# Key block 3 as one score tile over both query halves, and four value-product visits a quad in place of six

## The reference

```python
kv_c = x @ W_kv; kv_c = kv_c * rsqrt(mean(kv_c**2) + EPS) * g_kv
q_c = x @ W_q
k_content, v = heads(kv_c @ W_kdec, 16), heads(kv_c @ W_vdec, 16)
q_content = heads(q_c @ W_qdec, 16)
k_rope, q_rope = heads(x @ W_krope, 32), heads(q_c @ W_qrope, 32)   # both rotated by cos/sin
q, k = concat(q_content, q_rope), concat(k_content, k_rope)         # 16 heads of 48
scores = einsum('bhqd,bhkd->bhqk', q, k) * 48 ** -0.5               # causal mask over 1024 x 1024
out = einsum('bhqk,bhkd->bhqd', softmax(scores), v) @ W_o
```

## Time and profile before

| | us |
|---|---|
| median of 3 runs | 1963.67 |
| lowest, highest | 1953.01, 1965.78 |
| the profiled execution: its own time | 1961.27 |
| its span in the profile | 1959.6 |
| TensorE (PE) busy | 1901.9 (97%) |
| VectorE (DVE) busy | 1434.8 (73%) |
| ScalarE (ACT) busy | 1013.1 (52%) |
| GpSimd (POOL) busy | 858.1 (44%) |

### The profile page before, as it was taken

The page is one execution under the profiler, slowest core; times in us unless marked ns, Lnnn a source line. Parts: engine busy times, 40 slices in busy tenths (PEclk is TensorE's granted clock), DMA queues, the critical chain, the costliest instruction groups (busy, mean ns, idle before and its releaser), DMA issues.

```text
span 1959.6 us, 32772 instructions
## 1 busy us (share of the span) xinstructions
PE 1901.9 (97%) x11102; PEld 1337.0 (68%) x11102; DVE 1434.8 (73%) x4570; ACT 1013.1 (52%) x2125; POOL 858.1 (44%) x912
## 2 busy tenths in 40 slices
PE   8789999999999999999999999999999999999997
PEld 7546666767767676776767677677766777677556
DVE  5667777777777777877877777777778778677632
ACT  3435565555555555555555555545555555554551
POOL 3456454543445435355452545535444543432121
PEclk9879999999999999999999999999999999999999
DMA  3775675676775656766666676755677566665611
GB/s 104 199 191 155 166 188 151 151 187 167 176 177 129 178 149 159 200 157 153 162 164 152 179 189 156 179 149 153 153 189 178 143 158 174 167 147 129 133 41 44
DMA packets 169767, 307.50 MB, mean 157 GB/s; under 512 B 15104, under 2 KB 33792, under 8 KB 169600
## 3 DMA queue, kind: packets, MB, share of 16 engines
q1 hardware_dynamic: 169600, 305.40, 62.3%
HBM read 178.99 MB, written 126.22 MB: 156 GB/s over the span
## 4 chain that ended last, share of the span: by engine, by line
PE 86%; DVE 8%; ACT 3%; issue 2%; DMA 1%; POOL 1%; SPq 0%; POOLq 0%; DVEq 0%
PE st_b L775 15%; PE mx_b L807 15%; PE st_b L777 13%; PE o_b L795 13%; PE tp_b L843 5%; PE wj_b L732 5%; PE tp_b L840 4%; PE wj_b L719 3%; PE wj_b L701 3%; PE wj_b L734 2%; PE wj_b L712 2%; PE wj_b L741 1%; PE wj_b L747 1%; DVE mx_b L998 1%; ACT probs L884 1%
## 5 line engine op out<-in xcount | busy, mean ns | idle before, releaser
L884 ACT ACTIVATE probs<-st_b 128x512 f32<-128x512 f32 (+3 forms) x1536 | 699.6, 490 | 582.2 <-PE st_b L777 535.8
L998 DVE CUSTOM_DVE_ANT_0 mx_b<-mx_b,tri 128x256 f32<-128x256 f32 (+3 forms) x1024 | 510.6, 516 | 123.8 <-PE mx_b L807 120.5
L775 PE MATMUL st_b<-st 97*128 97x512 f32 (+2 forms) x1536 | 587.7, 388 | 8.5 <-ACT probs L884 5.0
L807 PE MATMUL mx_b<-st 96*128 96x256 f32 (+2 forms) x1536 | 543.2, 400 | 23.8 <-DVE mx_s L998 14.3
L777 PE MATMUL st_b<-st,k_st 96*128 96x512 f32 (+2 forms) x1536 | 531.2, 350 | 0.0
L1001 DVE TENSOR_REDUCE mx_s<-mx_b 128x1 f32<-128x512 f32 (+1 forms) x512 | 334.3, 653 | 131.8 <-PE mx_b L807 126.5
L1199 POOL TENSOR_SCALAR_AFFINE_SELECT probs<-probs 128x512 f32<-128x512 f32 x256 | 172.2, 677 | 538.1 <-ACT probs L884 538.0
L807 PEld LDWEIGHTS mx_b<-st 96*128 96x128 f32 x1536 | 280.9, 192 | 181.1 <-issue 73.4
L775 PEld LDWEIGHTS st_b<-st 97*128 97x128 f32 x1536 | 291.4, 190 | 123.8 <-issue 54.7
L777 PEld LDWEIGHTS st_b<-st,k_st 96*128 96x128 f32 x1536 | 294.2, 192 | 37.1 <-issue 13.9
L795 PE MATMUL o_b<-probs,v_s 128*17 128x512 f32 (+3 forms) x3072 | 290.3, 496 | 0.0
(11 more groups left out here) (198 smaller groups left out, 2332.7 us busy)
## 6 DMA issues: line engine op xcount, KB each, us to landing
st<-q_scratch SPq DMA_DIRECT2D x128, 384.0 KB, 6.0
st<-k_scratch SPq DMA_DIRECT2D x128, 384.0 KB, 8.7
k_st<-k_scratch SPq DMA_DIRECT2D x128, 384.0 KB, 9.2
q_scratch<-hi_t SPq DMA_DIRECT2D x32, 768.0 KB, 3.8
q_scratch<-lo_t SPq DMA_DIRECT2D x32, 768.0 KB, 5.3
k_scratch<-hi_t SPq DMA_DIRECT2D x30, 768.0 KB, 6.1
k_scratch<-lo_t SPq DMA_DIRECT2D x30, 768.0 KB, 4.9
ao_scratch<-o_f SPq DMA_DIRECT2D x252, 32.0 KB, 1.8
```

The lines of the kernel that those rows point to most:

```text
L775: nc.tensor.matmul(dst, k1_st[u][0:SHIFT + 1, a, P * j:P * j + P], q_st[u][0:SHIFT + 1, a, q0:q0 + w], start=True, stop=False)
L807: nc.tensor.matmul(mx_b[:, m % 2, 0:w], q_st[u][0:SHIFT, a, P * i:P * i + P], k1_st[u][0:SHIFT, a, k0:k0 + w], start=True, stop=True).then ...
L884: nc.scalar.activation(probs[:, a, PLACE[s]:PLACE[s] + n], st_b[:, a % 2, HALF - n:HALF], ACT.Exp, scale=SCALE).then_inc(exp_done, 1)
L998: nc.vector.tensor_tensor_reduce(src, src, tri[:, HALF - n:HALF], 1.0, NEG, ALU.add, ALU.max, dst).then_inc(mx_done, 1)
```

## The change

1. The tile of key block 3 in half 0 is widened from 128 to 256 columns (queries 384 to 639, so over the edge of the two halves), and the tile of key block 3 in half 1 shrinks from 512 to 384 columns (queries 640 to 1023). That second tile is moved up from place 7 to place 5, behind the tile of key block 0 in half 1. The 12 tiles have now 512, 384, 256, 256 | 512, 384, 512, 512, 512, 384, 256, 128 columns; the sum stays 4608.
2. PV has four visits: tiles (0, 1, 2, 3), (4, 5), (6, 7, 8), (9, 10, 11). The new list TAKES says what a visit multiplies. The part of tile 3 that belongs to half 1 (128 columns) is multiplied in the second visit, after tile 4, which starts the sums of that half. So tile 3's place in the ring is free only after the second visit (PV_OF).
3. The first score of tile 3 now waits for the shift of half 1 as well (shift_in[u][1]).
4. The last job's first output products wait in addition until o_b is read and all exponentials are done.
5. All order tables are new. TensorE's has 3940 letters (head 1120, batch 478 four times, tail 908) with the same S, X, F, J, P; 128 V in place of 192, 45 d in place of 68.

```diff
+BOTH = HT - 1
 ATT = []
 for h2 in range(2):
     for j in range((h2 + 1) * HT):
         q0 = max(P * j, HALF * h2)
-        ATT.append((h2, j, q0, HALF * (h2 + 1) - q0, q0 == P * j))
+        if j == BOTH:
+            q0 += P * h2
+        ATT.append((h2, j, q0, HALF * (h2 + 1) - q0 + (P if j == BOTH and not h2 else 0), q0 == P * j))
+
+at = [s for s in range(len(ATT)) if ATT[s][0] and ATT[s][1] == BOTH][0]
+ATT.insert(HT + 1, ATT.pop(at))
...
-PV = [(s, s + 1) for s in range(0, NS, 2)]
+PV = [(0, 1, 2, 3), (4, 5), (6, 7, 8), (9, 10, 11)]
 NV = len(PV)
-PV_OF = [p for p in range(NV) for _ in PV[p]]
-PV_END = [max(p for p in range(NV) if ATT[PV[p][1]][0] == h2) for h2 in range(2)]
+TAKES = []
+for p in range(NV):
+    takes = [(s, ATT[s][0], ATT[s][2], min(ATT[s][3], HALF * (ATT[s][0] + 1) - ATT[s][2])) for s in PV[p]]
+    if HT in PV[p]:
+        takes.insert(1, (BOTH, 1, HALF, P))
+    TAKES.append(takes)
+PV_OF = [max(p for p in range(NV) if s in [take[0] for take in TAKES[p]]) for s in range(NS)]
+PV_END = [max(p for p in range(NV) if ATT[PV[p][-1]][0] == h2) for h2 in range(2)]
...
                     if late and k == 0:
                         pe.wait_ge(ao_early, 16)
+                        pe.wait_ge(o_read, 2 * QUADS)
+                        pe.wait_ge(exp_done, UNITS * QUADS)
...
                     if j == 0 and a == 0:
                         pe.wait_ge(shift_in[u][h2], 16 * (g // 2 + 1))
+                    if s == BOTH and a == 0:
+                        pe.wait_ge(shift_in[u][1], 16 * (g // 2 + 1))
...
-                    for s in PV[p]:
-                        h2, j, q0, n, _ = ATT[s]
+                    for s, h2, q0, n in TAKES[p]:
+                        j, place = ATT[s][1], PLACE[s] + q0 - ATT[s][2]
                         for a in range(HQ):
                             last = nc.tensor.matmul(o_b[32 * a:32 * a + DV + 1, 0, q0 - HALF * h2:q0 - HALF * h2 + n],
-                                                    v_s[g // NQ % 2][:, j, HQ * q + a, :], probs[:, a, PLACE[s]:PLACE[s] + n],
+                                                    v_s[g // NQ % 2][:, j, HQ * q + a, :], probs[:, a, place:place + n],
                                                     start=(j == 0), stop=(s == PV[PV_END[h2]][-1]))
```

More of the change, by code:

```diff
@@ L150 @@
[L150 to L159, removed]
@@ new lines @@
+        "JXSSXXJXSXSJXSXSPSXSXVXSXSPSXSXFXSSXPSXSXPSXSXVSXSXPSXSXPSXSXSSXSSXXSXSFXSSXPSXSXPXSXSJXSXSJXSXSJXSXSJXX"
+        "VXXPSSXVXSXSXSXSXSXSXSXSJXSSXJXSXSJXSSXVFSSXXSSXXSSSXSXVSXSXJSXSJXSSXJXSXSJXSXSPSXSXFSXSXPSXSXJXSXSXPXSS"
+        "XXJXSXSJXSXSVXXPSXSXVXSXSPXSXSXJXSXSJXSXSJXSXSJXSSPSVSFSXXSPSXSXPSXSXJSXSXJSXSXJSXSXPSXSXPSXSXVSFSSPXSXS"
+        "XSSXPXSXSXVXSXSXPXSXSPSXSXSVXSXSJXSXSXJXSJXSXSJXSXSXSXSXSSVXSXSXSSXJSXSJFSXSXJSX",
+        "SXSXVXSXSXSXSXSXSXSSSXSXSSJSSXJXSSXJFXSXSXJXSXSPXSXSPXSXSJXXPVXXJXSXSJXSXSVXSXSPXSXSXPXSXSPSXSXJSXSXJSSJ"
@@ new lines @@
+        "XSXSJXSXSPXXSSXFXSSXVXXPVSXSXJSXSPXSXSJXSXSJSXSXPSXSXFSXSXPSXSXSXSPXSXSSXSXXSXSVXJXSJXSXSJXSXSJXSXSXVXSX"
+        "SXPXSXSPXSXSJXSXSJFSSXJSXSXVSXSXSXSXSXSXSVSXSXJSXSXJSSXJXSXSJFSXSXPSXSXPSXSXJXSXSXPXSSXXJXSXSJXSXSVXXPSX"
+        "SXVXSXSPXSXSXJXSXSJXSXSJXSXSJXSSPSVSFSXXSPSXSXPSXSXJSXSXJSXSXJSXSXPSXSXPSXSXVSFSSPXSXSXSSXPXSXSXVXSXSXPX"
+        "SXSPSXSXSVXSXSJXSXSXJXSJXSXSJXSXSXSXSXSSVXSXSXSSXJSXSJFSXSXJSX",
+        "SXSXVXSXSXSXSXSXSXSSSXSXSSJSSXJXSSXJFXSXSXJXSXSPXSXSPXSXSJXXPVXXJXSXSJXSXSVXSXSPXSXSXPXSXSPSXSXJSXSXJSSJ"
@@ new lines @@
+        "CEEJEEEEHECEECEECEEJEEJEEJEEHEJEJEECEECEEEEJEECEEEEEECCEEEEEEEEEHEEEECEEEEECEEJJEECJEEHEEJEECEEJEECEEEEC"
+        "EEEEEEHEECEECEEEEEEEECEEJEEJEHEJEECEEEECEEJEECEEJCEEEECEEEEHEECEEJEEEEEEEECEECEEEEEEEEEEEHEEEEEEEJEEJEEJ"
+        "EEJEECEEEEJEEEEEEEECEEEECEEEEEEHEECEEEEEEEEJEEJEEJEEJEEJEECEEJEEEEHEECEEEECEEEECEECEEEECEECEEEEEEEEHEECE"
+        "ECEEJEEJEEJJHJEECEEEEEEEEEEJEEEEEEEEEEEEEEEEJEEJEEJEEJEECEEEECEEJEECEEEEHEECEEEECEEJEEJEEJEEJEEHEJCEEECE"
+        "ECEEJEEEEEECEECEEEEECEEEEHEECEECEECEEEEEJEHEEJJEEJEEEEEEJEEEEJEEEE",
@@ new lines @@
+        "EEEEEEEEEEEEEEEJEEJEEJEEJEECEECJCEEEHEEEEECEECEECEEJEEJEEJEEJHEECEEJEECEEJEECEEEEEECEEEECEEEEEEHEEEEJEJC"
+        "EEJEEJEJEEECEECEEJEEEEHEEEEEEEEEEEJEEJEEJEEJEECEECEEJEECEEEEHEECEEEECEEJEEJEEJEEJEEHEJCEEECEECEEJEEEEEEC"
+        "EECEEEEECEEEEHEECEECEECEEEEEJEHEEJJEEJEEEEEEJEEEEJEEEE",
+        "EEEEEEEEEEEEEEEJEEJEEJEEJEECEECJCEEEHEEEEECEECEECEEJEEJEEJEEJHEECEEJEECEEJEECEEEEEECEEEECEEEEEEHEEEEJEJC"
+        "EEJEEJEJEEECEECEEJEEEEHEEEEEEEEEEEJEEJEEJEEJEECEECEEJEECEEEEHEECEEEECEEJEEJEEJEEJEEHEJCEEECEECEEJEEEEEEC"
@@ L211 @@
+        "EECEEEEECEEEEHEECEECEECEEEEEEHEEEEEEEEEEEEEJEJEJEEJEEEEJEEEEEEEEEJEEEEEEEEEEEEEEEEEEEEEEEEEEEEJEEJEEJEEJ"
+        "EEJEEEEEJEEEEEEEEEEEEEEEEEEEEEEEEEEEEEEEEEEEEEEEEEEEEEEEEEEEEEEEEEEEEEEEEEEEEEEEEEEEEEEEEEEEEEEEEEEEEEEE"
+        "EEEEEEEEEEEEEEEEEEEEEEEEEEEEEEEEEEEEJJEEJJEEEEJEEEJjjjjjj",
     ),
@@ new lines @@
+        "MMMMLJoMMoJoMoMMMMMMMMMMJMMJMMMMfMJnMMJMMJMMJJMMJooMoMoMMLMMfLMMJnMMJMMoMMooMMoMMMMMMJJJJJJMMJJJJMMMMMMJ"
+        "MMJMMMMLLMMfMMnMMMMMMooMJMJMMJoMMoMMLfMMnMMLJMMJMMMMMMMMMMJJJJoMMJoMJoJoMMJMJMMJMMLMMLMJMMJMMfJJJnMMJMMJ"
+        "MMooMoMoMMMMMMMJfMMnJMMMMMJMMMLMMJMMLMMJJJMMJoooMMJJMMoMMMMMMMMMMJfJJJJJLJLnMMJJJMMMMMMJMMJMMMMMMfonoooM"
+        "MLMMMMLMJJMJMMoJMMJMMoLooMMMMMMLMMMJMMJMMJJJJJJJJMMMMMfJnMMJ",
+        "MJMMJoMMJMoMMJMMJMMoMMoMfnMMMMMJMMJMMMMJLoMMooJMMoLMMJJJMMJMJMMJMMMMLMMMMMMfJMMJnMMJJMJLJJJMMJJooMoMMoMM"
@@ new lines @@
+        "JMMJMMfMMnMMMLMMJJJMMMMJMMJLMMoMMooMMoMJMMJJJJMJMMJJJJMMMMLMMfJnMJMMJJLJMMMMJMMJoMMooMMoMMMfnMMJMMJMMMJM"
+        "MMLMMJMMLMMJJJMMJoooMMJJMMoMMMMMMMMMMJfJJJJJLJLnMMJJJMMMMMMJMMJMMMMMMfonoooMMLMMMMLMJJMJMMoJMMJMMoLooMMM"
+        "MMMLMMMJMMJMMJJJJJJJJMMMMMfJnMMJ",
+        "MJMMJoMMJMoMMJMMJMMoMMoMfnMMMMMJMMJMMMMJLoMMooJMMoLMMJJJMMJMJMMJMMMMLMMMMMMfJMMJnMMJJMJLJJJMMJJooMoMMoMM"
+        "JMMJMMfMMnMMMLMMJJJMMMMJMMJLMMoMMooMMoMJMMJJJJMJMMJJJJMMMMLMMfJnMJMMJJLJMMMMJMMJoMMooMMoMMMfnMMJMMJMMMJM"
@@ L262 @@
+        "sJqskasuusuaqkJusqsakJJssuuaqkusuksqJsasJuuauuqkss",
+        "qJkasJJsuauqkuqsuaskJsJsuuaqkssJuuqaksJJsuuaqkusuksqJsasJuuauuqkss",
+        "qJkasJJsuauqkuqsuaskJsJsuuaqkssJuuqaksJJsuuaqkusuksqJsasJuuaJuuqksqskaJsJsJaqkqsaksJJssaqkqsaksssaksskaa"
+        "JjjaJj",
     ),
```

125 lines of the change are left out of this document (28 added, 97 removed).

## The result

| us | before | after |
|---|---|---|
| median (lowest to highest, runs) | 1963.82 (1953.01 to 1965.78, 6) | 1949.16 (1944.84 to 1952.39, 6) |
| the profiled execution: time, span | 1961.27, 1959.6 | 1944.84, 1943.1 |

The account below looks back on a forecast made before the run. TensorE's own instruction stream was taken as the bound. The terms -15 - 20.5 + 0.9 + 0.65 = -34 us took the profiled 1961.3 to 1927.3, carried as 1928 us; range 1912 to 1949.

Parts of the forecast that it names:

- Part 1: Tiles of key block 3: 256 TensorE score matmuls 128 columns shorter, 15 us off; masks and row maxima unchanged.
- the ScalarE sum: ScalarE's exponentials of the two key block 3 tiles: 873 ns before, 877 after, counted as nothing.
- Part 2: Value products on TensorE: six visits a quad become four, 64 fewer at 0.32 us each, 20.5 us off.
- A further group of tiles: Added tile group within visits: 0 to 0.065 us each, taken as 0, with 10 us kept at the range's upper end.
- Part 3: New letter order on TensorE: 0.9 us for leaving other work, 0.65 us more in the tail, alternation 0.
- rival D: Alternating scores and row maxima removes a third of TensorE's 57.7 us idle time, 19 us: 1908 us; chance 0.07.
- Part 4: Added waits on tile 3's shift, its mask and the last job: taken as 0, upper bound 3 us.
- A: Visit cost of 0.32 us belongs to tile groups or returns as gaps, only the tiles' gain remains: 1948 us; chance 0.08.
- B: VectorE takes over in stretches as longer visits empty the row maxima banks; half the gain returns as waits: 1944; chance 0.09.
- C: First visit waits for tile 3's mask in GpSimd's queue, stopping TensorE; at 2 us a quad 1991 us; chance 0.03.
- The ring: Places of exponentials: the first visit must free tile 6's; tightest cover before the third score 0.86 us; taken as 0.
- the sign of being wrong: TensorE idle time on L775 or L807 behind ScalarE, VectorE or a DMA growing by more than 15 us.

Follow-up runs that it names:

- e1: New score tiles, TAKES and waits on the kernel before, with six visits and the old order tables except the front of quad 0: 1959.11 us, 0.9992.
- e4: Changed kernel with row maxima and scores in pairs again, XSXS written XXSS at 400 places of TensorE's table: 1966.48 us, 1.003 to the kernel before.
- e2: Changed kernel (new tiles, four visits) on the old order, only TensorE's V letters moved: 2140.01 us, 1.0932 to the kernel before.
- e3: Changed kernel in its new order with six visits of two tiles, 64 V letters put back: 2185.01 us, 1.1121 to the kernel before.
- both cuts: Exponentials and row maxima over half their columns from quad 2 on: kernel before 1931.26 us (0.9842), changed kernel 1919.59 us (0.9787).

## Why the prediction was wrong, point by point

**Part 1, the tiles: right in size, 15 us.** The distances are 0.235, 0.177 and 0.12 us as forecast, and the distances of e1 are 15 us shorter in sum. But alone it brings no gain that can be measured: "Masks and row maxima stay as they are" and the ScalarE sum, right as durations, say nothing of when a bank comes free.

**Part 2, the visits: right.** One slip: the four-tile visit has 1280 columns, not 1408, since tile 3's other 128 go with the second visit; it takes 2.28 us, by the same line. A further group of tiles costs nothing like 0.065 us.

**Part 3, the letters: not confirmed.** I took 0 for alternation and gave it a chance of its own downward, rival D, which didn't come. But e4 costs 17 us, so in these tables alternation does give something, mostly by fewer held matmuls (17 us of cost; the idle time of e4 is only 5 us larger) and not by taking from the 57.7 us of idle time as I had thought. With the pairs of e4 the whole gain is gone. That the measured time is still below before rests in part on a term that I had put at nothing.

**Part 4 is the step that failed.** "I take 0, with 0.1 us a quad or 3 us as the upper bound of an ordinary miss": I asked only whether a new wait would be long, and took for granted that all old waits stay. In its place the traces have 23 us in held matmuls, 151 more of them, 0.7 us a quad. The mechanism that I lacked is that a matmul costs 0.1 us as soon as its release comes at its turn. The two banks keep the exponential and the maximum two letters ahead; that more of them come just in time where the stream between becomes shorter is my reading, which e1 bears out (28 more) and no run isolates. By releaser, the exponentials' share rose by 11 us, that of the row maxima by 7, that of the evacuations of the projections' bank by 4.

**The rivals.** A's time, 1948, was the nearest. Its first half, that the constants aren't the visit's, is excluded by the rows of the visits; its second, that they "come back as gaps because the work behind is not ready any sooner", says in words what happened, and I gave the two together 0.08. B (1944, half of the gain back as waits) had the sum nearly right. Its mechanism is only a part: VectorE is the releaser of a third, and taking half of its maxima away left the pair closer together, not wider. C did not come in the change; the first visit stands 1.35 us (median) behind its mask, and TensorE idled before two of the 128 visits for a mask, 0.9 us in all. The ring isn't it either, although it changed as Part 4 feared. ScalarE waited for visits as follows, before (first row) and after:

```profile
ACT probs L884 <- PE o_b L795: 29.6, 12, 4.0
```

```profile
ACT probs L860 <- PE o_b L771: 63.0, 27, 4.0
```

That is ScalarE waiting 33 us more for TensorE, while TensorE's own waits behind these visits are some 0.03 us in the mean.

**What I had named as the sign of being wrong** (idle time on the score and maxima lines up by 15 us) did not show: it went from 32.3 to 32.7. Two other signs did: busy time is down by 17.6 in place of 34, and two visits show waits on the masks, though only 0.9 us. A wait that is shorter than the overlap of two matmuls is counted as busy, so idle time can't find it.

**What is shown and what is open.** Shown: the counted gain is in the stream; some 23 us come back in matmuls released just in time; the changed kernel has more of these at four loads of the other engines and at three orders of TensorE's table. Not shown: that the gain would be there without them, for no version got rid of them, and why just these letters. That a shorter stream under unchanged chains of two banks makes more of them is argued, with e1 for it; a third bank of st_b or mx_b wasn't tried. No version that does all of the work beat the changed kernel.

## What to carry to other kernels

Where TensorE is the bound and each step waits on a bank that two steps share, count what carries a wait and how far ahead its release comes, not only how long the waits are: each one that is released less than 0.1 us ahead costs up to 0.1 us behind it, beside what it is late itself. The page's idle and busy times don't show this loss; start-to-start times do, and here it took more than half of what the stream was cut by. An order found on a replay of one trace is a conjecture until it has run, even where the replay meets that trace within 1%.

## What the runs showed of the hardware that was not expected

- A matmul that starts at its release makes the next one 0.104 us late, however short its own wait; with 0.05 us of lead this is 0.05, from 0.11 us on nothing (the table above, for scores behind exponentials; for row maxima only the first of these is shown). The rows at 790.78 and 791.11 show one.
- Where TensorE waited more, its granted clock was lower, so that waits cost more than their length. The mean was 0.984 in the kernel before, 0.953 in e2 and 0.939 in e3 (above), where visits stood for masks and matmuls for maxima. Of spans of 1959.6, 2141.9 and 2193.9 us this takes an estimated 31, 101 and 134 us. With both cuts in the changed kernel it was 0.992 (1913.7 us of span). The Trainium skill, page "TensorE: Matmul & The Clock Gate", section "HAM oscillation — how this bites in real kernels", tells of a kernel whose clock falls in each wait for a DMA; the runs agree in so far as the clock is lower with more waits, here for masks and maxima.
- The price of going into the four column groups is one per visit, 0.13 us inside and 0.1 on either side, for two tiles and for four alike. The 0.1 behind a visit is of the same size as behind a held matmul; whether it is the same thing, no run shows.
- Two exponentials back to back overlap by 0.10 us. In the changed order more of them stand alone, and ScalarE's busy time grew by 25.6 us with the same work; in e4 it is 1009.5 us again, at a slower kernel.
